# Two layers of attention and feed-forward on one core: fewer shared-network steps in the routing stage, more in the combining stage, and their rounding on ScalarE

## The reference

```
x = x + norm(linear_attention(norm(x)))
x = x + norm(moe(norm(x)))
x = x + norm(window_attention(norm(x)))
x = x + norm(feed_forward(norm(x)))

def moe(x):
    scores = softmax(x @ gate_w.T)            # 16 experts
    combine = the two best scores, elsewhere 0
    h = silu(x @ w_gate[e]) * (x @ w_up[e])   # inner size 176, per expert
    y = sum over e of combine[:, e] * (h @ w_down[e])
    gu = x @ shared_gate_up                   # shared network, inner size 352
    return y + (silu(gu[:, :352]) * gu[:, 352:]) @ shared_down
```

## Time and profile before

| | |
|---|---|
| median of 3 runs | 1209.95 us (1207.2 to 1211.4) |
| profiled execution, its own time | 1203.83 us |
| its span, first to last instruction | 1201.9 us |
| PE busy | 1135.6 us (94%) |
| DVE busy | 755.8 us (63%) |
| ACT busy | 513.5 us (43%) |
| POOL busy | 240.4 us (20%) |
| mean granted PE clock | 0.971 |

### The profile page before, as it was taken

How to read it: one execution, slowest core, us unless ns; L and a number is a source line. 1 busy time by engine, 2 the same in 40 slices (tenths; PEclk the granted TensorE clock), 3 DMA queues, 4 the chain that set the end, 5 groups by cost and what they waited for, 6 DMA issues and landing times. The chain is left out here.

```text
span 1201.9 us, 19841 instructions
## 1 busy us (share of the span) xinstructions
PE 1135.6 (94%) x7044; PEld 993.0 (83%) x7044; DVE 755.8 (63%) x1599; ACT 513.5 (43%) x969; POOL 240.4 (20%) x274
## 2 busy tenths in 40 slices
PE   5999999999999999999999995899998869989997
PEld 4988989988989889888898994677776768878897
DVE  4765665665656647557567478664445976686656
ACT  6576344344443443344434555432222356554322
POOL 1112010110100101101001002033332742322221
PEclk9999999999999999999999997899999968999999
DMA  4001001000001001001000003633333324000001
GB/s 149 10 1 36 10 1 36 9 0 35 9 0 39 5 0 44 0 1 43 0 0 1 1 1 132 216 92 106 106 106 92 96 79 145 1 1 1 19 18 36
DMA packets 29197, 50.33 MB, mean 42 GB/s; under 512 B 5107, under 2 KB 19411, under 8 KB 27859
## 3 DMA queue, kind: packets, MB, share of 16 engines
q1 hardware_dynamic: 25106, 38.81, 9.9%
q0 software_dynamic: 3840, 10.49, 3.4%
q10 hardware_dynamic: 192, 0.26, 0.1%
HBM read 36.70 MB, written 10.49 MB: 39 GB/s over the span
## 5 line engine op out<-in xcount | busy, mean ns | idle before, releaser
L635 POOL TENSOR_TENSOR linear_out_row<-linear_out_row,lin_sq 128x512 f32<-128x512 f32 x64 | 91.2, 1426 | 599.7 <-ACT lin_sq L536 596.8
L42 PE MATMUL lin_bank<-keep_xT_hi,lin_w_hi 128*128 128x512 f32 x384 | 155.1, 404 | 2.6 <-DVE keep_xT_lo L244 2.6
L591 DVE TENSOR_TENSOR lin_st<-lin_bank,lin_mask 128x512 f32<-128x512 f32 x64 | 44.2, 691 | 175.7 <-PE lin_bank L446 175.7
L43 PE MATMUL lin_bank<-keep_xT_lo,lin_w_hi 128*128 128x512 f32 x384 | 152.4, 397 | 0.0
L44 PE MATMUL lin_bank<-keep_xT_hi,lin_w_lo 128*128 128x512 f32 x384 | 152.2, 396 | 0.0
L532 ACT ACTIVATE lin_o<-lin_bank 128x512 f32<-128x512 f32 x64 | 38.3, 598 | 191.5 <-PE lin_bank L477 191.5
L473 PE MATMUL lin_bank<-lin_st,lin_v 128*128 128x128 f32 x512 | 94.0, 275 | 0.0
L42 PEld LDWEIGHTS lin_bank<-keep_xT_hi,lin_w_hi 128*128 128x128 f32 x384 | 72.8, 190 | 17.9 <-issue 3.0
L477 PE MATMUL lin_bank<-lin_qd,lin_state 128*128 128x128 f32 x448 | 87.2, 276 | 0.0
L44 PEld LDWEIGHTS lin_bank<-keep_xT_hi,lin_w_lo 128*128 128x128 f32 x384 | 72.4, 189 | 17.7
L43 PEld LDWEIGHTS lin_bank<-keep_xT_lo,lin_w_hi 128*128 128x128 f32 x384 | 72.6, 189 | 14.7
(11 more groups left out here) (378 smaller groups left out, 2821.8 us busy)
## 6 DMA issues: line engine op xcount, KB each, us to landing
lin_raw<-in_wp SPq DMA_DIRECT2D x8, 1024.0 KB, 4.8
sorted_y<-shared_loaded SPq DMA_DIRECT2D x48, 128.0 KB, 2.1
experts_up_expert_up<-in_wgu SPq DMA_DIRECT2D x16, 352.0 KB, 7.3
keep_x<-in_x SPq DMA_DIRECT2D x4, 512.0 KB, 7.4
lin_raw_out<-in_wop SPq DMA_DIRECT2D x8, 256.0 KB, 2.7
tokens_x<-linear_out_row SPq DMA_DIRECT2D x4, 512.0 KB, 10.2
linear_out_row<-in_ffn_up SPq DMA_DIRECT2D x2, 1024.0 KB, 6.1
tail_q<-tail_qT SPq DMA_DIRECT2D x28, 64.0 KB, 2.0
```

The lines of the kernel that those rows point to most:

```text
L42: nc.tensor.matmul(out, lh, rh, start=first, stop=False, skip_group_check=skip)
L43: nc.tensor.matmul(out, lh, rl, start=False, stop=False, skip_group_check=skip)
L591: dve.tensor_tensor(C4(st[:, a, :]), C4(bank[2 + a][:]), mask[:, a:a + 1, :].broadcast_to([P, TPS, P]), ALU.mult).then_inc(st_sb, 1)
L635: pool.tensor_tensor(part, part, sq[:, a, :], ALU.add).then_inc(squares_sb, 1)
```

## The change

`SHARED_EARLY` becomes 1. The routing stage keeps three steps (group 0), the combining stage has nine (groups 1 to 3), and these use the form with ACT's rounding. Two semaphores for it are made in `moe_keep`. In the routing stage PE's last logits come ahead of the shared products, the rank products ahead of the down products, and both token products directly one behind the other. The last two loads of down weights wait for the second gather instead of the second token product. In the combining stage tile 4 now waits for group 1's output, and the bank for the tail of the turned tiles changes from 2 to 3.

```
-SHARED_EARLY = SEGS // 2
+SHARED_EARLY = 1
...
                 work.sp_load(sp, expert_down, 12, 14)
-                sp.wait_ge(router.tokens_mm, 2)
+                sp.wait_ge(work.xs_in[1], DMA)
                 work.sp_load(sp, expert_down, 10, 12)
...
                 net.dve_rest(dve, *STEPS[1])
-                net.dve_rest(dve, *STEPS[2])
                 router.dve_slots(dve, chain)
-                net.dve_product(dve, *STEPS[3])
                 router.dve_row_one_hot(dve, 0)
                 router.dve_token_one_hot(dve, chain, 0)
-                net.dve_rest(dve, *STEPS[3])
                 router.dve_row_one_hot(dve, 1)
                 router.dve_token_one_hot(dve, chain, 1)
-                net.dve_product(dve, *STEPS[4])
-                net.dve_product(dve, *STEPS[5])
+                net.dve_rest(dve, *STEPS[2])
                 router.dve_tokens(dve, chain)
-                net.dve_rest(dve, *STEPS[4])
                 router.dve_passed(dve, chain)
-                net.dve_rest(dve, *STEPS[5])
                 router.dve_tiles(dve, chain)
...
                 net.act_round(act, *STEPS[2])
-                net.act_step(act, *STEPS[3])
-                net.act_round(act, *STEPS[3])
                 net.act_output(act, 0)
-                net.act_step(act, *STEPS[4])
-                net.act_step(act, *STEPS[5])
-                net.act_round(act, *STEPS[4])
-                net.act_round(act, *STEPS[5])
-                net.act_output(act, SHARED_EARLY - 1)
...
-                    if g == L:
-                        net.pe_up(pe, *STEPS[0])
                     pe.wait_ge(norms.low, KT * (g + 1))
                     router.pe_logits(pe, g)
                 router.pe_turn(pe, L)
+                net.pe_up(pe, *STEPS[0])
                 net.pe_up(pe, *STEPS[1])
                 net.pe_up(pe, *STEPS[2])
+                router.pe_ranks(pe)
                 net.pe_down(pe, *STEPS[0])
-                router.pe_ranks(pe)
-                net.pe_up(pe, *STEPS[3])
                 net.pe_down(pe, *STEPS[1])
-                net.pe_up(pe, *STEPS[4])
+                router.pe_tokens(pe, 0)
+                router.pe_tokens(pe, 1)
                 net.pe_down(pe, *STEPS[2])
-                router.pe_tokens(pe, 0)
-                net.pe_up(pe, *STEPS[5])
-                router.pe_tokens(pe, 1)
-                net.pe_down(pe, *STEPS[3])
-                net.pe_down(pe, *STEPS[4])
-                net.pe_down(pe, *STEPS[5])
...
             net.split_before = True
+            net.product_sb, net.rounded = keep.late_product, keep.late_rounded
...
-                net.dve_step(dve, chain, *STEPS[0])
-                net.dve_step(dve, chain, *STEPS[1])
-                weigh(a, 0, 1)
+                net.dve_product(dve, *STEPS[0])
+                net.dve_product(dve, *STEPS[1])
+                net.dve_rest(dve, *STEPS[0])
+                weigh(a, 0)
+                net.dve_rest(dve, *STEPS[1])
+                weigh(a, 1)
                 weights.dve_low(dve)
+                net.dve_product(dve, *STEPS[2])
+                net.dve_rest(dve, *STEPS[2])
                 weigh(a, 2)
-                net.dve_step(dve, chain, *STEPS[2])
-                weigh(a, 3, 4)
+                net.dve_product(dve, *STEPS[3])
+                net.dve_rest(dve, *STEPS[3])
+                weigh(a, 3)
+                net.dve_product(dve, *STEPS[4])
+                net.dve_rest(dve, *STEPS[4])
+                weigh(a, 4)
                 a.dve_known(dve, chain, "y")
-                net.dve_step(dve, chain, *STEPS[3])
+                net.dve_product(dve, *STEPS[5])
+                net.dve_rest(dve, *STEPS[5])
                 a.dve_x_by_tile(dve, chain)
-                net.dve_step(dve, chain, *STEPS[4])
+                net.dve_product(dve, *STEPS[6])
+                net.dve_rest(dve, *STEPS[6])
                 a.dve_apply(dve, "x", a.by_dve, a.z_dve)
-                net.dve_step(dve, chain, *STEPS[5])
+                net.dve_product(dve, *STEPS[7])
+                net.dve_rest(dve, *STEPS[7])
                 weigh(b, 0, 1)
+                net.dve_product(dve, *STEPS[8])
+                net.dve_rest(dve, *STEPS[8])
                 a.dve_low(dve, turned)
...
+                net.act_round(act, *STEPS[0])
+                net.act_round(act, *STEPS[1])
                 weights.act_high(act)
-                for step in STEPS[2:5]:
-                    net.act_step(act, *step)
-                net.act_output(act, SHARED_EARLY)
+                net.act_step(act, *STEPS[2])
+                net.act_round(act, *STEPS[2])
...
+                net.act_step(act, *STEPS[4])
+                net.act_round(act, *STEPS[4])
+                net.act_output(act, 1)
+                net.act_step(act, *STEPS[5])
+                net.act_round(act, *STEPS[5])
                 a.act_apply(act, "y", range(a.n))
-                net.act_step(act, *STEPS[5])
+                net.act_step(act, *STEPS[6])
+                net.act_round(act, *STEPS[6])
+                net.act_step(act, *STEPS[7])
+                net.act_round(act, *STEPS[7])
+                net.act_output(act, 2)
                 a.act_apply(act, "x", (0, 1, 4))
+                net.act_step(act, *STEPS[8])
+                net.act_round(act, *STEPS[8])
                 a.act_high(act, turned)
```

More of the change, by code:

```diff
@@ L1081, in feed_forward @@
         after = AddNorm(c, keep, "after", y, keep.spare, keep.last_added)
-        own, pool_own, stored = c.sem("own"), c.sem("pool_own"), keep.stored
+        own, pool_own, stored = keep.ffn_own, c.sem("pool_own"), keep.stored
         J = net.J
@@ L1763, in moe_keep @@
 def moe_keep(keep, c):
+    keep.ffn_own, keep.late_product, keep.late_rounded = c.sem("ffn_own"), c.sem("late_product"), c.sem("late_rounded")
     keep.weight1, keep.weight2 = c.sb("weight1", [P, TT]), c.sb("weight2", [P, TT])
@@ L2032, in window_attention @@
         NJ, NB = len(JOBS), len(JOBS) // BATCH
-        kv_bank, q_bank, v_bank, tail_bank = (bank[0:2], turned), (bank[2:4], turned), (bank[5], bank[7]), (bank[2], bank[5])
+        kv_bank, q_bank, v_bank, tail_bank = (bank[0:2], turned), (bank[2:4], turned), (bank[5], bank[7]), (bank[3], bank[5])
         rows = lambda b, half, n=1: slice(b * 2 * GD + half * GD, b * 2 * GD + (half + n) * GD)
@@ L2271, in _ @@
                 net.act_step(act, *STEPS[1])
+                net.act_round(act, *STEPS[0])
+                net.act_round(act, *STEPS[1])
                 weights.act_high(act)
-                for step in STEPS[2:5]:
-                    net.act_step(act, *step)
-                net.act_output(act, SHARED_EARLY)
-                a.act_apply(act, "y", range(a.n))
-                net.act_step(act, *STEPS[5])
+                net.act_step(act, *STEPS[2])
+                net.act_round(act, *STEPS[2])
+                net.act_step(act, *STEPS[3])
+                net.act_round(act, *STEPS[3])
+                net.act_step(act, *STEPS[4])
[3 more added lines that the diff above has]
+                net.act_round(act, *STEPS[5])
+                a.act_apply(act, "y", range(a.n))
+                net.act_step(act, *STEPS[6])
[3 more added lines that the diff above has]
+                net.act_output(act, 2)
                 a.act_apply(act, "x", (0, 1, 4))
+                net.act_step(act, *STEPS[8])
+                net.act_round(act, *STEPS[8])
                 a.act_high(act, turned)
```

## The result

The changed kernel took 1218.21 us (median of seven executions, 1214.52 to 1220.74 but for one of 2635.28, which stands alone, is unexplained and is in no comparison). The kernel before took 1208.29 in the same comparison (seven executions). The ratio is 1.0068 (1.0054 to 1.0082), so the change costs 8.2 us, between 6.5 and 9.9; the two medians differ by 9.9. I had forecast 1214.3 and a loss of 4.4.

The account below looks back on a forecast made before the run. VectorE's chain bounds the routing stage and VectorE's queue the combining stage, with TensorE close behind there. Routing −2.9 and combining +7.3 sum to +4.4, added to the median 1209.95 for 1214.3 us; range 1208.5 to 1218.5.

Parts of the forecast that it names:

- Last logits, choice: Routing stage: last logits moved ahead bring the scores 1.5 us earlier, of which the choice gains 0.5.
- Slots to token list: Routing stage: shared work leaves VectorE's queue, second token product at half clock; token list 2.2 us earlier in all.
- First gathers: Routing to experts: first gather lands after 2.9 us with fewer loads beside it; experts start 3.9 earlier (2.7 to 4.5).
- Clock, +1.0: Experts' start: TensorE's longer pause ahead is paid back in low clock, costing 1.0 us (bounds 0 to 2).
- Combining, VectorE: Combining stage: nine split steps add work and waits on VectorE; first arrange 7.3 us later (6.1 to 9).
- Combining, TensorE: Combining stage: three more steps add 12.7 us of TensorE work, partly filling gaps; key/value projection 7.4 later.
- the routing gain of 2.9: Routing in all: experts' start 3.9 us earlier less 1.0 for the clock, so −2.9 (−4.5 to −0.7).
- A: Rival on both stages: full routing gain of 4.5, combining costs only TensorE's 6.1; net +1.6 us, chance 0.15.
- B: Rival at the first attention jobs: denser work keeps full clock, half-clock stretch shrinks by 4.75; net −0.4 us, chance 0.08.
- C: Rival at the experts' start: late down-weight loads cost TensorE 2 us, clock loss 2; net +7.4, chance 0.12.
- D: Rival: split works without waits, or routing gains more than seen; net −4 us, chance 0.08.

Follow-up runs that it names:

- Experiment 10: Kernel before with last logits ahead of the first shared product and the last two weight loads released by the second gather's landing; 1203.16 us, ratio 1.0007.
- experiment 11: Kernel of experiment 10 with the shared work of steps 3 to 5 put behind the token tiles; 1203.15 us, ratio 1.0017 to before.
- experiment 9: Changed kernel with the nine combining steps rounded on VectorE again, on chip C; 1205.83 us, ratio 1.0040 to before.
- experiment 3: Kernel before with only TensorE's last logits and turn moved ahead of the first shared up product, chip A; 1209.13 us, ratio 0.9981.
- experiment 12: Kernel of experiment 3 timed again on chip D; 1209.38 us, ratio 0.9999 to before.

## Why the forecast was right in sign and too low

- **Last logits, choice.** Held. Common point to the scores' first reduction: 10.07 in the first profile of before (whose earlier logits ran at 0.63 a row, not 0.40), 8.8 in four others with the old order, 7.3 in every profile with the new. So 1.5 earlier; the choice ends 0.4 earlier (19.61 to 19.19). I had 1.5 and 0.5.
- **Slots to token list.** Held roughly. The list comes 35.0 after the common point in the old order and 33.5 in the change (34.4 in its first profile): −1.5 for my −2.2. The token products took 1.44 each; I had priced only the second at half clock, and the first lost its 0.57 too.
- **First gathers.** Held: 3.0 to 3.1 from first gather to first turn in all five profiles with the changed routing, 5.8 to 6.3 in the five with that of before. The experts start 4.1 earlier (43.48 to 39.38), forecast 3.9. Most of it comes from the two loads that wait longer. Experiment 10 has 2.7 of it without giving up three steps, gives 1.1 back in the experts' stage, and shows no gain in its times.
- **Clock, +1.0.** The reason failed, and that the size came near is luck. The experts' stage is longer by 0.7 (123.96 to 124.68, B to C). But once the experts had started the clock was low for 4 us in both kernels: here before again (B) and the change again (C), windows with PE's busy time first and the granted clock after POOL's:

```profile
800.00:804.00 4.00, 4.00 (x10) 2.38 (x10) 0.34 (x1) 0.70 (x2) 2.18 (x3) 0.58 0.22 66
```

```profile
794.00:798.00 4.00, 4.00 (x11) 2.54 (x10) 0.34 (x1) 1.08 (x3) 2.82 (x4) 0.55 0.74 204
```

  A pause of TensorE ahead of the experts was there before and is there now, and is paid once either way. With two loads later and six shared steps (experiment 10) the windows of the experts' start read 1.00 throughout, and the stage took 125.10 all the same. What differs in the second line is the DMA share, 0.74 for 0.22: in the change SyncE issues the last two loads from 793.62 on, 0.5 ahead of the first up product, in before again from 790.79 on, 9.0 ahead. That they make the stage longer is shown for experiment 10 (the wait on DMA at 801.10); for the change it is inferred.
- **Combining, VectorE.** Held, once the profile is free of the stall. Waits of the rests 6.54, where I had 5.9 for the round trips and 0.9 for roundings 3 and 4. First arrange 54.46 after the stage's start, +7.9 over the first profile of before, +6.1 over the second, and +7.2 over the old stage on the same chip (47.29 and 47.28, experiments 10 and 11); forecast +7.3, 6.1 to 9.
- **Combining, TensorE.** Held. In the stall-free profile it has three idles from its first product to the projection, 1.58 and two of under 0.7, and the projection comes 42.7 after the first product; I had 41.8. That TensorE alone holds most of the loss is what experiment 9 shows: with the rounding back on VectorE it has no idle left, and the stage still takes 53.12, 5.8 more than with six steps on the same chip. The half-clock stretch went, as I had it: the mean granted clock to the projection is 1.00.
- **What I overlooked: the gap to the median.** I saw that the profile of before was 6.1 below the median of its timed executions and simply added the change to the median, without asking what the 6.1 were. Most likely they were an event in the combining stage that the profile did not hold: in the first profile of the change and in every one from chips A and D, VectorE and ScalarE stand for 4 to 10 until 21 us after the stage's first product, also in the old stage (experiments 3 and 12). Before itself was not profiled there, so this is inferred. In the profiles the edited stage pays more for it: 61.64 and 65.46 against 54.9 with the old stage, +6.7 and +10.5, where stall-free pairs give +6.1 to +7.9.
- **The missing 3.8 (8.2 for 4.4) stays open.** The stall cannot be all of it, for on chip C, without the stall, the ratio still says +7.1 (4.5 to 9.9) and the medians +5.8. There the parts of two profiles (B and C) sum to +3.6 from the common point on: −4.1, +0.7, +6.1, +0.9. So 2.2 to 3.5 are in no part that I can name. What can be said: beside the kernel of experiment 10 on the same chip the parts are −1.4, −0.4, +7.2 and −0.5, together +4.9, and the medians differ by just that (1208.01 and 1203.16). The piece that fails to add up is thus the one from before to experiment 10, where the profiles say that routing and experts gain 1.6 (−2.7 + 1.1) and the times say nothing is gained. That points to the routing gain of 2.9 as the term that was too good; it is not shown, since before was not profiled on chip C.
- **Rivals.** A (routing −4.5 without clock loss, combining +6.1, net +1.6) is out by the times, and the quiet profiles' +3.6 lies nearer to my +4.4 than to it. B is out: the clock in the first attention jobs stayed at about half (0.51 from 968 to 990 on chip C). C: the first expert down product of the change came 7.3 after the up product on chip C, 6.5 in before again, 7.6 and 6.0 in the first profiles, so 0.7 to 1.6 of the 2 that I gave to late down weights is the most that it can be. D is out: each rest that stands right behind its product waits.

The Trainium skill, "Perfetto Trace Analysis", Optimizing Scalar/DVE Operations, says that handing some work to ScalarE may make sense when VectorE is saturated. The runs speak against it for this chain: with nothing between product and rest the hand-over costs 0.77 and saves a cast of 0.43 (0.57 by the spacing of the steps), and VectorE's own rounding was 1.3 (stage) to 2.2 (medians) faster on chip C.

## What to carry to other kernels

Before adding a change to a median, ask why the profiled execution is off that median; a gap of 6 us in 1200 may be an event in the very stage that is edited, and a second profile of the unchanged kernel, on another chip if there is one, is the cheapest experiment. Splitting a chain over two engines did not pay here, where mostly nothing stands between its parts: price the round trip from a row where nothing does, and ask which engine is full in that stage before relieving one. A transfer that is moved away from one wait should be looked for at the next one. And a gain that profiles of single executions show between two chips should be timed on one before it enters a sum.

## What the runs showed of the hardware

- Chips differ by as much as this change (or the times of measuring do; the two were not told apart). The kernel before took 1201.7 and 1202.2 on chips B and C, 1210.2 and 1209.3 on A and D, and 1208.3 in the first comparison. In all five profiles from A and D and in the first one of the change (three with the changed routing and three with six shared steps there, rounding on either engine), an engine that waits for TensorE's products is released 21.0 to 21.1 after the combining stage's first product, after an idle of 4.3 to 10.1 marked "remote", although TensorE's rows have the product done up to 8.1 earlier. None of the other eight profiles has it.
- What does it is not settled. It ends 3.0 to 3.6 after the start of the last of GpSimd's first fourteen row gathers (17.5 to 18.0 after the first product in all six), and in five of the six TensorE puts two matmuls 1.3 to 1.4 apart while it lasts. That points to the gathers. But the same gathers run at the same time in quiet profiles of the old stage (17.5 and 18.0), and the data moved is alike: from 10 to 22 after the first product 98, 100 and 66 GB/s in stretches of four on chip B, 98, 98 and 66 on A with the stall. The two runs that held gathers back were made on a chip without the stall, so they tell nothing. It was not tried on a chip that has it.
- The round trip from VectorE's product over ScalarE's rounding back to VectorE was 0.77 of idle to the hundredth in all five bare cases of one profile, for 96 and 128 partitions alike. I had read 0.84 from the routing stage, so such a number could be carried from one stage to another within 0.1.
